# Joints of the last stages of a two-layer transformer kernel: who waits for scatters, which queues write the zero rows, when table words are loaded, and the first gathers of the second attention

## The chip, the cores and the metric

The kernel runs on one core of one Trainium2 chip. The core's engines are TensorE (PE in the profile, with PEld for its weight loads), VectorE (DVE), ScalarE (ACT), GpSimd (POOL) and SyncE (SP). An engine name with a q (POOLq, SPq) means the engine's own queue of instructions: its waits, branches, register loads and DMA issues. The metric is the time of one execution on the device in microseconds (us); lower is better.

## The reference

The input x is 8 sequences of 512 tokens of 128 floats. Four stages are added to it, each on its layer norm:

```python
x = x + attn0(ln(x))   # 16 heads of 8; sum of a windowed (128), a strided (4) and a full softmax, times 1/3, @ w_out
x = x + ffn0(ln(x))    # 7 experts of 512, top 2 per token (SwiGLU), plus one shared expert for all tokens
x = x + attn1(ln(x))   # 16 heads of 8, rotary q and k, causal softmax, @ W_out
x = x + ffn1(ln(x))    # 8 experts of 256, top 2 per token, one after the other:
# gates = softmax(x @ gate_W + gate_b); e1, e2 = top-2 experts of a token, with weights w1, w2
# o1 = relu(x @ W1[e1] + b1[e1]) @ W2[e1] + b2[e1];  boost = x + 0.5 * o1
# o2 = the same of boost with expert e2;  result = layernorm(x + w1 * o1 + w2 * o2) * gamma + beta
```

## The kernel before

The program is a row of blocks. Each block has one instruction list for each engine; between blocks stands a joint: every engine runs to the end of its list and executes a DRAIN, all meet at a barrier, GpSimd clears the block's semaphores, and all meet again. These instructions carry the line of the block's `with nc.cleanup_on_exit()`: L60 for an attention, L1585 for the routing of the first mixture, L1974 for its expert pass, L2147 for each of the two expert passes of the second mixture.

The order of the blocks is: setup; attention 0; routing and shared expert of mixture 0 (`route_and_share`); its expert pass over 70 blocks of 128 token rows (`routed_pass`); attention 1, which also routes mixture 1 (`attention(..., causal=True, due, gate)`); expert pass 0 and expert pass 1 of mixture 1 (`expert_pass`, r = 0 and 1), 39 blocks of 128 rows each.

**Attention 1.** Events for all engines are written out in one list (`order`); `walk` gives each engine the events for which it has a handler, so each engine meets them in that order. It works on 8 sequences, b = 0 to 7, each as 4 tiles of 128 tokens and 4 groups of heads. Before sequence b is normed, the two expert results of each of its tokens are added to X: GpSimd issues one gather with add for each tile t and each of the two results j (`early` for b = 0, 1 and the first half of 2; `results` later). j = 1 of a tile may start only when j = 0 of that tile has landed. Before the change the wait stands ahead of the four gathers of j = 1 and asks for all four of j = 0:

```python
def early(b, turn, j):
    if j:
        pool.wait_ge(s_yg[b], 16 * NT)
    for t in range(NT):
        ...
```

The list begins with early(0,0), two memsets on VectorE (`ones`, L604 and L606), early(0,1), the norm of b = 0, early(1,0), early(1,1), the preparation of q, k and v for b = 0, the norm and the preparation of b = 1, and only then the first score maxima (`smax`, on TensorE and VectorE) and the slots of the pipeline.

**Routing of mixture 1.** For each sequence: `g_norm` (VectorE statistics, GpSimd's power, L1147 and L1149), `g_shift` (VectorE, L628), `g_rows` (ScalarE: one activation that writes token numbers, L993, and four that write the normed rows, L996), `g_beta` (GpSimd, L1157: X plus beta into the same row buffer), `g_turn`, `g_logits`, `g_soft`, `g_count`, `g_place`, `g_put`, and `scatter`, one indirect DMA for each tile from GpSimd into the DRAM tensor `rows_1` (L1175). For b = 0 to 6 these lie between the slots; for b = 7 they come one after the other at the end. `finish` then pads each expert's last block: SyncE loads eight addresses into registers and issues eight writes of 128 zero rows (L1240, L1241), waits for them and for the weights (L1242, L1243), VectorE makes the table of blocks, and GpSimd waits for its scatters (L1180).

**Expert passes.** SyncE reads the 128 rows of block i (L2203) and, in pass 0, now and then a block of zero rows for pass 1 (L2206). TensorE transposes them, ScalarE copies the expert's weights and the transposed rows (L2253, L2255), TensorE multiplies (L2229), ScalarE and VectorE apply the relu, TensorE multiplies again (L2237, L2240), VectorE combines (L2319, L2323, L2325; in pass 1 also the layer norm, of which the last step is L2311), and GpSimd scatters the rows to their places (L2333), in pass 0 into `rows_2` and in pass 1 into the output. Which expert a block has stands in a table in SBUF, four blocks to a word. `words` loads all ten words into registers ahead of the loop, on TensorE, ScalarE and, in pass 0, VectorE (`value_load`, L2180: a TENSOR_LOAD, register operations and an assertion each). In pass 0 VectorE also makes the table of pass 1, in parts, one in each of the first iterations (`next(later, None)`, all shown at L1411). At the end of a pass GpSimd waits for its scatters, one semaphore for each of the 16 row buffers (L2345).

**`routed_pass`** of mixture 0 loads its words inside the loop: one in every fourth iteration, on TensorE, ScalarE and VectorE, ahead of the weight copies (L2057, L2076).

## Time and profile before

| | |
|---|---|
| median of 3 runs | 1601.72 us (1600.91 to 1602.95) |
| profiled execution, its own time | 1599.95 us |
| its span, first to last instruction | 1598.2 us |
| attention 0 | about 15 to 626 us |
| mixture 0, routing and pass | 626 to 749 and 749 to 953 us |
| attention 1 with routing | 953 to 1452 us |
| expert pass 0, expert pass 1 | 1452 to 1524 and 1524 to 1598 us |
| busy share: PE, DVE, ACT, POOL | 86%, 67%, 56%, 41% |
| mean granted TensorE clock | 0.94 |

A row of the timeline gives the start in us, how long the instruction (or the run of xN instructions) took in us, the engine, the line, the operation with its output and inputs, and in brackets how long the engine sat idle before it and what released it. "issue" means that it waited for nothing that the profile shows. A row of the view of one line gives the shortest, median and longest duration in ns and the first and the last start in us. DRAIN, EVENT_SEMAPHORE and TENSOR_LOAD rows belong to an engine's queue and are not counted as busy.

### The profile page before, as it was taken

How to read it: one execution, taken by the hardware profiler on the slowest of the kernel's cores; microseconds unless marked ns; L12 is line 12 of the kernel's file. 1: busy time of each engine (PE TensorE's matmuls, PEld its weight loads, DVE VectorE, ACT ScalarE, POOL GpSimd, SP SyncE). 2: the span in 40 equal slices, each digit the busy share in tenths (PEclk: the TensorE clock that was granted, in tenths of full speed). 3: DMA queues.
4: the chain of work that ended last, by engine and by line, in shares of the span. 5: the costliest groups of instructions: out<-in, count | busy, mean ns of one | idle time of the engine just before them, and what ended most of it. 6: DMA issues, size and time to landing. Idle time of an engine off the chain costs nothing. (4 is left out here: it accounts for less than half of the span.)

```text
span 1598.2 us, 36810 instructions
## 1 busy us (share of the span) xinstructions
PE 1377.7 (86%) x12519; PEld 924.5 (58%) x12646; DVE 1068.3 (67%) x2710; ACT 894.7 (56%) x1594; POOL 654.2 (41%) x984
## 2 busy tenths in 40 slices
PE   2799999999999997998999972899999999944866
PEld 1255555555555554766999971355555555534866
DVE  4678778787877763674444444677787887844656
ACT  1567676767767665622444430366666666632666
POOL 2223332323333222055333326656667553342736
PEclk8699999999999998999999995799999999976978
DMA  4211212112121102350111113333433222205653
GB/s 128 66 42 38 59 41 63 53 37 63 35 59 43 62 6 92 90 85 14 49 50 48 49 33 55 84 82 70 113 79 102 71 89 72 68 35 157 213 144 106
DMA packets 91848, 113.65 MB, mean 71 GB/s; under 512 B 13075, under 2 KB 75570, under 8 KB 91538
## 3 DMA queue, kind: packets, MB, share of 16 engines
q1 hardware_dynamic: 74930, 89.74, 19.9%
q0 software_dynamic: 16736, 21.55, 5.7%
q8 instruction: 106, 1.74, 0.5%
q14 instruction: 76, 0.62, 0.1%
HBM read 71.78 MB, written 38.95 MB: 69 GB/s over the span
## 5 line engine op out<-in xcount | busy, mean ns | idle before, releaser
L522 DVE TENSOR_REDUCE wm<-wsm 128x16 f32<-128x512 f32 x512 | 330.1, 685 | 112.4 <-PE wsm L770 109.5
L956 ACT ACTIVATE we<-wst 128x1024 f32<-128x1024 f32 x320 | 325.1, 1023 | 119.9 <-PE wst L803 109.1
L518 DVE TENSOR_REDUCE cnm<-csm 128x1 f32<-128x512 f32 (+3 forms) x352 | 213.8, 637 | 49.4 <-PE csm L767 47.2
L956 ACT ACTIVATE ce<-cst 128x896 f32<-128x896 f32 (+1 forms) x256 | 173.7, 699 | 113.9 <-PE cst L798 75.5
L770 PE MATMUL wsm<-wks,wqs 96*128 96x512 bf16 x512 | 172.1, 391 | 9.8 <-DVE wm L522 6.2
L763 PE MATMUL csm<-cks,cqs 96*128 96x256 bf16 (+3 forms) x512 | 131.8, 309 | 13.8 <-DVE cnm L518 10.1
L803 PE MATMUL wst<-wqs,wks 128*128 128x512 bf16 x417 | 128.3, 383 | 13.3 <-issue 12.0
L2033 PE MATMUL abup<-abxt,abws 128*128 128x128 f32 x1120 | 138.5, 278 | 0.4 <-ACT abxt L2059 0.4
L2033 PEld LDWEIGHTS abup<-abxt,abws 128*128 128x128 f32 x1120 | 132.4, 194 | 0.7 <-ACT abxt L2059 0.7
L837 PE MATMUL woa<-we,wv 128*32 128x128 f32 (+2 forms) x2560 | 130.5, 340 | 0.0
L1058 POOL TENSOR_TENSOR wdif<-wglb,wloc 128x16 f32<-128x16 f32 x32 | 7.1, 221 | 289.7 <-DVE wloc L544 289.7
L2081 DVE TENSOR_TENSOR abht<-absg,abup 128x512 f32<-128x512 f32 x70 | 48.1, 688 | 101.6 <-ACT absg L2064 101.6
L795 PE MATMUL cst<-cqs,cks 128*128 128x384 bf16 (+3 forms) x480 | 112.4, 296 | 2.7 <-ACT ce L956 0.7
L2097 POOL DMA_INDIRECT axb<-rows,asource x67 | 66.1, 986 | 117.2 <-DVE abys L2088 112.7
L1131 POOL TENSOR_SCALAR_AFFINE_SELECT ce<-ce 128x256 f32<-128x256 f32 x128 | 65.3, 539 | 92.8 <-ACT ce L956 92.5
L770 PEld LDWEIGHTS wsm<-wks,wqs 96*128 96x128 bf16 x512 | 49.7, 98 | 88.0 <-DVE wm L522 51.7
L2064 ACT ACTIVATE absg<-abup 128x512 f32<-128x512 f32 x70 | 41.8, 597 | 102.5 <-PE abup L2033 102.5
L837 PEld LDWEIGHTS woa<-we,wv 128*32 128x32 f32 x2560 | 66.8, 109 | 52.7 <-issue 36.4
L763 PEld LDWEIGHTS csm<-cks,cqs 96*128 96x128 bf16 x512 | 45.8, 101 | 76.3 <-DVE cnm L518 43.2
L767 PE MATMUL csm<-const_b 128*128 128x128 bf16 (+2 forms) x352 | 88.0, 250 | 0.0
L829 PE MATMUL coa<-ce,cv 128*32 128x512 f32 (+3 forms) x1024 | 82.7, 441 | 0.7 <-ACT ce L956 0.6
L803 PEld LDWEIGHTS wst<-wqs,wks 128*128 128x128 bf16 x512 | 39.7, 101 | 63.1 <-ACT we L956 25.4
(330 smaller groups left out, 3012.3 us busy)
## 6 DMA issues: line engine op xcount, KB each, us to landing
wqs<-qk_parts SPq DMA_DIRECT2D x96, 96.0 KB
wks<-qk_parts SPq DMA_DIRECT2D x96, 96.0 KB
cqs<-qk_parts SPq DMA_DIRECT2D x96, 96.0 KB
cks<-qk_parts SPq DMA_DIRECT2D x96, 96.0 KB
b1r<-rows SPq DMA_DIRECT2D x39, 194.0 KB, 2.7
qk_parts<-wpt SPq DMA_DIRECT2D x48, 128.0 KB
qk_parts<-cpt SPq DMA_DIRECT2D x48, 128.0 KB
b0r<-rows SPq DMA_DIRECT2D x39, 130.0 KB, 2.5
```

Source lines behind the costliest of these rows:

```text
L518: dve.tensor_reduce(NM[:, n % 2, first:first + heads, t], got, AX.X, ALU.max).then_inc(s_mx, 1)
L522: dve.tensor_reduce(M[:, n % 2, hs, t, :].rearrange("p (w f) -> p w f", f=DIL), SM[:, j % 2, :].rearrange("p (w i f) -> p w f i", w=NT, f= ...
L763: pe.matmul(sm[:, i * keys:(i + 1) * keys], QS[0:MR0, h, t * P:(t + 1) * P], KS[0:MR0, h, 0:keys], start=(i == 0), stop=False, skip_group_ ...
L767: pe.matmul(own, const["later_b"], ident, start=False, stop=True, skip_group_check=True).then_inc(s_sm, 1)
L770: pe.matmul(sm, QS[0:MR0, h, t * P:(t + 1) * P], KS[0:MR0, h, :], start=True, stop=True, skip_group_check=True).then_inc(s_sm, 1)
L795: m = pe.matmul(st[:, at:at + width], KS[:, h, kb * P:(kb + 1) * P], QS[:, h, kb * P:S], start=True, stop=not masked, skip_group_check=True)
L803: m = pe.matmul(st[:, c * S:(c + 1) * S], KS[:, h, kb * P:(kb + 1) * P], QS[:, h, :], start=True, stop=True)
L829: m = pe.matmul(OA[VW * hs:VW * (hs + 1), S - width:S], V[:, kb, g * HG + hs, 0:VW], E[:, e_slot(g, HG * r + hs), at:at + width], start=(k ...
L837: m = pe.matmul(span(OA[VW * hs:VW * (hs + 1), :], a, z), V[:, r, g * HG + hs, col:col + VW], span(e, a, z), start=(r == 0 and a == 0), st ...
L956: act.activation(E[:, e_slot(g, i), 0:width], ST[:, (U * g + i) % 2, 0:width], ACT.Exp, scale=SCALE).then_inc(s_ex, 1)
L2033: m = pe.matmul(UP[:, i % 2, w, c * P:(c + 1) * P], WS[:, i % 2, w, c * P:(c + 1) * P], XT[:, i % 2, :], start=True, stop=True)
L2097: pool.indirect_dma_start(XB[:, q, :], None, rows, bass.IndirectOffsetOnAxis(ap=source[:, i:i + 1], axis=0)).then_inc(s_in[q], 16)
```

## The change

Five edits are made.

1. Scatters: the waits for GpSimd's scatters at the end of attention 1, of pass 0 and of pass 1 move from GpSimd's list to SyncE's.
2. Zero rows: of the eight writes of `finish`, SyncE loads and issues the even four and ScalarE the odd four, on ScalarE's own DMA queue.
3. Words: four words (`SOON1`) are loaded ahead of the loop of an expert pass, the other six inside it, one at the head of each iteration until all ten are known, on TensorE, ScalarE and (pass 0) VectorE.
4. First gathers: for b = 0 and 1 a new semaphore for each tile, `s_y0[t]`, lets the j = 1 gather of tile t wait for the j = 0 gather of that tile alone. The counts that `norm_stats` and `results` wait for on `s_yg[0]` and `s_yg[1]` are lowered to match.
5. Routing rows: ScalarE writes the token numbers after the four row activations instead of before them, and `g_beta` on GpSimd waits for `g_shift` on VectorE as well.

```diff
@@ -151,6 +151,7 @@
             s_yg = [sem(f"yg{i}") for i in range(4)]
+            s_y0 = [sem(f"y0{t}") for t in range(NT)]
         if gate:
@@ -450,7 +451,7 @@
                 if due:
-                    dve.wait_ge(s_yg[b % 4], 16 * 2 * NT * (b // 4 + 1))
+                    dve.wait_ge(s_yg[b % 4], 16 * 2 * NT * (b // 4 + 1) - (16 * NT if b % 4 < 2 else 0))
                 if causal and b > 2:
@@ -990,12 +991,12 @@
                 room(act, b)
-                act.activation(ROWS[:, rows_of(b), IN_TOKEN].bitcast(U32), const["steps"][:, b * NT:(b + 1) * NT], ACT.Identity,
-                               bias=const["row"]).then_inc(s_gtok, 1)
                 for t in range(NT):
...
                 m.then_inc(s_grow, 1)
+                act.activation(ROWS[:, rows_of(b), IN_TOKEN].bitcast(U32), const["steps"][:, b * NT:(b + 1) * NT], ACT.Identity,
+                               bias=const["row"]).then_inc(s_gtok, 1)
 
@@ -1006,6 +1007,12 @@
                     act.activation(route.V[:, 0:T, :], route.V[:, 0:T, :], ACT.Exp).then_inc(s_gex, 1)
+
+            def finish(b, turn):
+                act.wait_ge(s_r, marks["padded"])
+                for e in range(1, NE1, 2):
+                    at = act.value_load(route.PAD[0:1, 0, e:e + 1], min_val=0, max_val=TOP * CAP - P)
+                    act.dma_start(gate.rounds[0][bass.ds(at, P)], gate.ZE[:, 0:IN_ROW]).then_inc(s_pad, 16)
 
@@ -1016,24 +1023,26 @@
                            rows=rows, scores=scores, evac=evac, heads_T=heads_T, g_rows=g_rows, g_turn=g_turn, g_soft=g_soft,
-                           g_put=g_put))
+                           g_put=g_put, finish=finish))
 
...
                 if j and t == 0:
-                    pool.wait_ge(s_yg[b % 4], 16 * 2 * NT * (b // 4) + 16 * NT)
+                    pool.wait_ge(s_yg[b % 4], 16 * 2 * NT * (b // 4) + (0 if b % 4 < 2 else 16 * NT))
                 at = bass.IndirectOffsetOnAxis(ap=due[0][:, j, b * NT + t:b * NT + t + 1], axis=0)
...
             def early(b, turn, j):
-                if j:
+                if j and b > 1:
                     pool.wait_ge(s_yg[b], 16 * NT)
                 for t in range(NT):
+                    if j and b < 2:
+                        pool.wait_ge(s_y0[t], 16 * (b + 1))
                     at = bass.IndirectOffsetOnAxis(ap=due[0][:, j, b * NT + t:b * NT + t + 1], axis=0)
                     pool.indirect_dma_start(X[:, b * NT + t, :], None, due[1], at, compute_op=ALU.add
-                                            ).then_inc(s_yg[b], 16)
+                                            ).then_inc(s_yg[b] if j or b > 1 else s_y0[t], 16)
 
@@ -1153,6 +1162,7 @@
                 pool.wait_ge(s_res, b + 1)
+                pool.wait_ge(s_gsh, b + 1)
                 room(pool, b)
@@ -1175,12 +1185,8 @@
 
-            def finish(b, turn):
-                for i in range(RING1):
-                    pool.wait_ge(s_sc[i], 16 * NT * len(range(i, B, RING1)))
-
             walk(pool, dict(results=results, early=early, fill=fill, norm_rows=norm_rows, join=join, left1=left1, left2=left2, vcopy=vcopy, sel=sel, maxima=maxima, scores=scores,
-                            loads=loads, g_norm=g_norm, g_beta=g_beta, g_put=g_put, scatter=scatter, finish=finish))
+                            loads=loads, g_norm=g_norm, g_beta=g_beta, g_put=g_put, scatter=scatter))
 
@@ -1236,10 +1242,12 @@
                 sp.wait_ge(s_r, marks["padded"])
-                for e in range(NE1):
+                for e in range(0, NE1, 2):
                     at = sp.value_load(route.PAD[0:1, 0, e:e + 1], min_val=0, max_val=TOP * CAP - P)
...
                 sp.wait_ge(s_gw, 16 * 7)
+                for i in range(RING1):
+                    sp.wait_ge(s_sc[i], 16 * NT * len(range(i, B, RING1)))
                 sp.wait_ge(s_pad, 16 * NE1)
@@ -1370,6 +1378,7 @@
 USED1 = 39
+SOON1 = 4
 RING1 = 3
@@ -2180,7 +2189,11 @@
         def words(eng):
-            return [word(eng, at) for at in range(-(-N // UN))]
+            return [word(eng, at) for at in range(SOON1)]
+
+        def more(eng, known):
+            if len(known) * UN < N:
+                known.append(word(eng, len(known)))
 
@@ -2206,6 +2219,8 @@
                 sp.wait_ge(s_pad, 16 * NE1)
+            for q in range(Q):
+                sp.wait_ge(s_out[q], 16 * len(range(q, N, Q)))
 
@@ -2218,6 +2233,7 @@
             for i in range(N + 1):
+                more(pe, known)
                 if i + 1 < N:
@@ -2245,6 +2261,7 @@
             for i in range(-1, N + 3):
+                more(act, known)
                 if i + 1 < N:
@@ -2279,6 +2296,7 @@
                 if not final:
+                    more(dve, known)
                     next(later, None)
@@ -2341,8 +2359,6 @@
                 scatter(i)
-            for q in range(Q):
-                pool.wait_ge(s_out[q], 16 * len(range(q, N, Q)))
 
```

## Rows read from the trace of the kernel before

**Rows 1.** Busy time by engine, of 100 us in the middle of attention 1.
```profile
1100.00:1200.00 100.00, 93.14 (x840) 54.71 (x845) 82.50 (x203) 63.15 (x113) 65.10 (x82) 1.00 0.36 90
```

**Rows 2.** Timeline of GpSimd, first gathers of attention 1.
```profile
963.09 1.53 POOL L1035 DMA_INDIRECT X<-results,slots  x1 [1.98 <-DMA X<-results,slots]
...
984.23 1.55 POOL L1035 DMA_INDIRECT X<-results,slots  x1 [2.09 <-DMA X<-results,slots]
...
990.54 1.55 POOL L1035 DMA_INDIRECT X<-results,slots  x1 [0.30 <-issue]
```

**Rows 3.** Timeline of VectorE in the same stretch.
```profile
959.37 6.88 DVE L606 MEMSET cks<- 64x8192 bf16 x1 [1.66 <-issue]
...
994.52 0.87 DVE L457 BATCH_NORM_STATS2 cstats<-X 128x6 f32<-128x128 f32 x4 [5.71 <-DMA X<-results,slots]
```

**Rows 4.** Line L628 over the whole run: count, durations in ns.
```profile
L628 DVE SCALAR_TENSOR_TENSOR cgsh<-cgmv,cgrs x8: 295/328/1158, 1091.3 to 1422.9; 128x4 f32<-128x4 f32 x8
```

**Rows 5.** Timeline, routing of the last sequence.
```profile
1422.80 1.25 POOL L1157 TENSOR_TENSOR brows<-X,bbe 128x512 f32<-128x512 f32 x1
1422.92 1.16 DVE L628 SCALAR_TENSOR_TENSOR cgsh<-cgmv,cgrs 128x4 f32<-128x4 f32 x1 [1.53 <-POOL cgrs L1149]
1424.11 0.30 ACT L993 ACTIVATE brows<-const 128x4 uint32<-128x4 f32 x1 [6.90 <-DVE cgsh L628]
```

**Rows 6.** Timeline, end of attention 1 and start of pass 0.
```profile
1436.94 8.98 SPq L1241 DMA_DIRECT2D rows<-bze  x8
...
1441.05 0.96 POOL L1175 DMA_INDIRECT rows<-brows,bIDX  x1 [0.31 <-issue]
...
1452.73 2.95 SPq L2203 DMA_DIRECT2D b0r<-rows  x4
```

**Rows 7.** Queue instructions of four joints, DRAIN on GpSimd, durations in ns.
```profile
L60 POOLq DRAIN  x1: 6591/6591/6591, 1444.1 to 1444.1; - x1
...
L2147 POOLq DRAIN  x3: 46/133/3244, 1519.4 to 1523.4; - x3
...
L1585 POOLq DRAIN  x3: 40/106/4800, 743.8 to 749.1; - x3
...
L1974 POOLq DRAIN  x3: 40/97/6711, 928.9 to 952.6; - x3
```

**Rows 8.** Timeline of GpSimd, the last indirect DMA ahead of three joints.
```profile
745.89 0.94 POOL L1962 DMA_INDIRECT axb<-rows,asource  x1 [0.30 <-issue]
...
929.10 0.94 POOL L2097 DMA_INDIRECT axb<-rows,asource  x1 [1.85 <-DVE abys L2088]
...
1516.69 0.98 POOL L2333 DMA_INDIRECT rows<-b0r  x1 [0.30 <-issue]
```

**Rows 9.** Line L2180 over the run: word loads of two engines, ns.
```profile
L2180 PEldq TENSOR_LOAD <-bTAB x20: 295/300/557, 1451.9 to 1529.6; - x20
...
L2180 DVEq TENSOR_LOAD <-bTAB x10: 297/304/450, 1451.9 to 1457.4; - x10
```

**Rows 10.** Timeline of TensorE, first transposes of the two passes.
```profile
1458.75 0.69 PE L2216 MATMUL b0tx<-const,b0r 128*128 128x128 f32 x2 [24.22 <-issue]
...
1530.20 0.68 PE L2216 MATMUL b1tx<-const,b1r 128*128 128x128 f32 x2 [17.86 <-issue]
```

**Rows 11.** Page, DMA issues: KB each, median us from issue to landing.
```profile
b1r<-rows SPq DMA_DIRECT2D x39, 194.0 KB, 2.7
...
b0r<-rows SPq DMA_DIRECT2D x39, 130.0 KB, 2.5
```

**Rows 12.** Timeline of VectorE in the pass of mixture 0, with and without a word.
```profile
806.52 0.43 DVE L2076 COPY abws<-awu 128x512 f32 x1 [0.42 <-issue]
...
808.81 0.42 DVE L2076 COPY abws<-awu 128x512 f32 x1
```

**Rows 13.** Timeline of GpSimd, where the unbroken run of scatters begins in each pass.
```profile
1472.83 0.99 POOL L2333 DMA_INDIRECT rows<-b0r  x1 [0.81 <-DVE b0r L2323]
...
1541.71 0.98 POOL L2333 DMA_INDIRECT out<-b1r  x1 [24.04 <-DVE b1r L2311]
```

## The prediction

> **What bounds the kernel now.** I read the busy time by stage first. In the middle of attention 1 TensorE is busy 93% of the time and VectorE 82% [rows 1]; the change removes nothing there. It touches the places where these engines stand still: the start of attention 1, the routing of the last sequence, the three joints and the first iterations of the passes. So I went through those with the timeline of all engines, asking which instruction ends last, and took the queue instructions of the joints line by line.
>
> At the start of attention 1 VectorE waits for the gathers: its statistics for b = 1 begin when the last gather has landed, after 5.71 us of idle time [rows 3]. At the end of attention 1 the zero-row writes are issued by 1436.94 + 8.98 = 1445.9, and the last scatter by 1442.0 [rows 6], but GpSimd's DRAIN runs from 1444.1 for 6.59 us, to 1450.7 [rows 7]. That DRAIN is what the joint waits for. The joint after pass 0 is alike: last scatter issued by 1517.7 [rows 8], DRAIN 1519.4 to 1522.6 [rows 7]. In the passes GpSimd sets the pace once it has caught up: from 1472.83 in pass 0 and from 1541.71 in pass 1 [rows 13] the scatters follow one another every 0.98 + 0.30 us or so without a break (34 and 38 intervals). Whatever comes earlier ahead of these two points comes earlier at the end of the pass.
>
> **Part 1, first gathers.** The fifth gather waited 1.98 us instead of the 0.30 of its neighbours, and in b = 1 2.09 us [rows 2]: 1.68 + 1.79 = 3.47 us of waiting on GpSimd. With a semaphore for each tile nothing of it should be left: a gather lands at most 4.0 us after it starts (990.54 to 994.52 [rows 2, 3]), and the gather that needs it comes four gathers later, at least 4 x (1.53 + 0.30) = 7.3 us. Queued behind the waits are the other gathers, the norm's power and the memset of v; all move up. VectorE's statistics for b = 1 wait for nothing but the last gather, so its norm, its projections and then the first maxima come 3.5 us earlier; b = 0 needs only 1.7 us of that, and its copies out and back lie ahead of the first maxima. I take 3.5; the bounds are 3.5 and 0, if the pipeline of attention 1 is paced by something that did not move. The new semaphores cost one wait each of a value already reached.
>
> The fifth gather now falls at 961.4, inside VectorE's memset (959.37 to 966.25 [rows 3]). The old one, at 963.09, did too, and took the same 1.53 us as those outside it [rows 2]. The Trainium skill (SBUF — State Buffer, "SBUF: two separate sides") says that GpSimd cannot write its DMA descriptors while VectorE holds the shared port pair in a 2-port mode. By that rule the fifth gather would stand until 966.25; the row of 963.09 does not show it for this memset. It is a rival below.
>
> **Part 2, routing rows.** `g_shift` takes 328 ns as a median of eight and 1158 ns once [rows 4]: the last time, when it runs beside GpSimd's L1157 (1422.80, 1.25 us) and ends with it [rows 5]. The added wait puts L1157 behind it: 1.16 - 0.33 = 0.83 us, on the path, since ScalarE's rows, the logits, the choice and the scatters of b = 7 all follow. The token numbers (0.30 us [rows 5]) go behind the rows: I take 0.2, as neighbouring ScalarE rows overlap; bounds 0 and 0.3. L1157's 1.25 us are hidden: the first use is the scatter at 1436.8, and GpSimd idles until then. For b = 0 to 6 `g_shift` stands seven events ahead of `g_beta`, so its wait is free. Sum 1.0 (0 to 1.1).
>
> **Part 3, zero rows on two queues.** Four writes instead of eight end SyncE's issuing near 1441 instead of 1445.9. GpSimd's DRAIN hides both; I count 0, for both bounds. Without that cover the edit would be worth up to 4.9 us. ScalarE has nothing else to do there.
>
> **Part 4, who waits for the scatters.** GpSimd reaches its DRAIN without waiting for landing. What does such a DRAIN take? Two joints show it [rows 7, 8]: the last gather ends at 746.83 and the DRAIN at 743.8 + 4.80 = 748.6, 1.8 us later, with 3 indirect DMAs in the block; and 930.04 to 928.9 + 6.71 = 935.6, 5.6 us later, with 67 in the block. Slope (5.6 - 1.8) / 64 = 0.059 us for each. The DRAINs behind a wait have the same slope: 6.59 us with 96 (64 gathers, 32 scatters), 3.24 with 39, 3.35 / 57 = 0.059. So I estimate 1.8 + 36 x 0.059 = 3.9 us after the last scatter's issue in a pass and 1.8 + 93 x 0.059 = 7.3 us in attention 1:
> - attention 1: 1442.0 + 7.3 = 1449.3 instead of 1450.7, 1.4 us;
> - pass 0: 1517.7 + 3.9 = 1521.6 instead of 1522.6, 1.0 us;
> - pass 1, which ends in the same way: 1.0 us.
>
> Sum 3.4. Lower bound 0, if the DRAIN's end hangs on the landing; upper bound, the old DRAIN directly behind the issue: 1448.6 and twice 1520.9, 2.1 + 1.7 + 1.7 = 5.5. SyncE's waits end where GpSimd's did, by 1444.1 and 1519.4, and lie under the DRAIN.
>
> **Part 5, words.** In pass 0 the first load starts at 1451.9 and VectorE's tenth at 1457.4, 0.61 us each [rows 9]; TensorE's ten end by 1458.75, 0.68 each [rows 9, 10]. With four words TensorE is ready at 1454.6; block 0's rows land at 1452.73 + 2.5 = 1455.2 [rows 6, 11]. Lead: 1458.75 - 1455.2 = 3.5 us. In pass 1 TensorE's last load starts at 1529.6 [rows 9], so the first at about 1523.7; the read comes 0.83 later as in pass 0 and lands after 2.7 [rows 11], at 1527.3: lead 1530.20 - 1527.3 = 2.9.
>
> Against it stand six loads in the loop. A word in a loop costs VectorE 0.42 us of idle time where it has none without [rows 12]. In pass 0 five of them (with `later`'s table work between) lie ahead of the fifth scatter, where the unbroken run begins: 5 x 0.42 = 2.1 if nothing absorbs them. VectorE still has small gaps there, so 1.7 are lost, and 1.8 are left (bounds 3.5, all hidden, and 3.5 - 5 x 0.61 = 0.4). In pass 1 VectorE has no words; on TensorE and ScalarE the loads lie behind multiplications and activations already issued. I take 0.1 us for each of five, 2.4 left (bounds 2.9 and 2.9 - 5 x 0.68 = -0.5).
>
> **Sum.** 3.5 + 1.0 + 0 + 3.4 + 1.8 + 2.4 = 12.1 us. The profiled execution's span becomes 1586.1 and its own time 1599.95 - 12.1 = 1587.8; the median of the runs is 1.8 above it, so 1589.6.
>
> **Rivals.**
> - *Loads in the loop cost in full (slower).* TensorE, ScalarE and VectorE hand each block on in a ring. If each load (0.68, about 0.6, 0.61) lies on that ring, five iterations cost 5 x 1.9 = 9.5 in pass 0 and 5 x 1.3 = 6.5 in pass 1, 16.0 against a lead of 6.4; with the other parts' 7.9 the sum is +1.7: 1603.4. It turns slower from about 1.4 us an iteration. Rows 12 speak against it. 4%.
> - *The start of attention 1 is absorbed*, by copies of q and k or by gathers of later sequences that pace it: 1593.1. TensorE's 93% speak against it. 15%.
> - *The words bring nothing*, because VectorE's table work in pass 0 and a later rise of TensorE's clock eat the lead: 1593.8. 12%.
> - *The moved wait does not do what it says*: DRAIN still ends a fixed time after landing: 1593.0. 8%.
> - *VectorE's memset holds back the early gather*: it starts at 966.25 instead of 963.09, 3.2 lost instead of 1.7 won: 1594.5. 2%.
> - Two of the middle three together: near 1597, 6%; all three: 1601, 4%.
>
> The forecast itself has 49%. A difference of 0.2% (3.2 us) is about what a measurement of this kernel can tell from no change. The cases above that bound are the first (4%, slower) and those within it the last one and part of the pairs (6%): faster 90%, same 6%, slower 4%. All bounds taken for the good give 3.5 + 1.1 + 5.5 + 3.5 + 2.9 = 16.5: 1585. The range reaches up to the pairs: 1585 to 1597.
>
> **What would show it.** The fifth gather near 961.4 with 0.30 idle, and statistics of b = 1 near 991. `g_shift` at 0.33 in all eight. GpSimd's DRAIN beginning before its last scatter has landed, ending 3.9 and 7.3 us after the issue. First transposes 3.5 us after the first word load instead of 6.9, and scatter five of pass 0 only 1.8 us closer to the barrier. The prediction is wrong if the slots of attention 1 do not keep the 3.5 us, if the DRAINs end as late as before, or if the first iterations of the passes stretch.

## The result and the profile after

| | before | after |
|---|---|---|
| median of the runs, us | 1601.72 | 1585.18 (5 runs, 1582.70 to 1587.47) |
| ratio, 95% interval | | 0.9895 [0.9881, 0.9909] |
| profiled execution, its own time, us | 1599.95 | 1585.6 |
| its span, us | 1598.2 | 1583.9 |

The change makes the kernel 16.8 us faster (1601.72 x 0.0105; 14.6 to 19.1 by the interval). The forecast was 12.1 us, and the 16.5 us of "all bounds for the good" come nearest. A second series of the changed kernel in another group of runs (e9 below) gave 1583.24 and 0.9887 [0.9872, 0.9901]. Two of the ten runs of e7 below had a mean granted clock of 0.901 instead of 0.944 and took 1593.9 and 1599.8 us, which widens its interval.

Start of attention 1: the timeline of GpSimd after the change, then that of VectorE, to be laid beside [rows 2, 3].

```profile
962.69 1.53 POOL L1044 DMA_INDIRECT X<-results,slots  x1 [0.30 <-issue]
...
982.14 1.82 POOL L1044 DMA_INDIRECT X<-results,slots  x1 [0.30 <-issue]
```
```profile
960.64 6.88 DVE L607 MEMSET cks<- 64x8192 bf16 x1 [1.66 <-issue]
...
992.39 0.87 DVE L458 BATCH_NORM_STATS2 cstats<-X 128x6 f32<-128x128 f32 x4 [4.95 <-DMA X<-results,slots]
```

Both waits of 1.98 and 2.09 us have become 0.30. The blocks ahead, which the change does not touch, end 1.27 us later in this execution, so 962.69 stands for the 961.4 of the prediction. The fifth gather lies wholly inside the memset and takes the same 1.53 us as its neighbours: the rival in which the memset holds it back is refuted here. The rule of the Trainium skill that the prediction named (SBUF — State Buffer, "SBUF: two separate sides") is for VectorE operations in a 2-port mode, and no row says that this memset is one. Had it held the port pair, the gather would have stood until 967.5.

Routing of the last sequence: the timeline of all engines after, beside [rows 5, 6].

```profile
1422.91 0.16 DVE L629 SCALAR_TENSOR_TENSOR cgsh<-cgmv,cgrs 128x4 f32<-128x4 f32 x1 [1.53 <-POOL cgrs L1158]
1423.11 1.65 ACT L995 ACTIVATE brows<-X,cgsh,cgrs 128x128 f32<-128x128 f32 x4 [5.72 <-DVE cgsh L629]
1423.21 1.27 POOL L1167 TENSOR_TENSOR brows<-X,bbe 128x512 f32<-128x512 f32 x1 [0.40 <-issue]
...
1434.51 0.25 POOL L1173 TENSOR_SCALAR brows<-bDEST 128x4 uint32<-128x4 f32 x1 [10.03 <-DVE bIDX L1420]
1435.89 1.08 POOL L1185 DMA_INDIRECT rows<-brows,bIDX  x1 [1.13 <-issue]
1437.27 1.26 POOL L1185 DMA_INDIRECT rows<-brows,bIDX  x1 [0.30 <-issue]
...
1440.40 0.96 POOL L1185 DMA_INDIRECT rows<-brows,bIDX  x1 [0.30 <-issue]
```

`g_shift` takes 0.16 us instead of 1.16, and GpSimd's addition starts behind it. From `g_shift` to the destinations the chain takes 11.60 us (1434.51 - 1422.91) instead of 12.76. The scatters then give part of it back: from the destinations to the start of the last one it takes 5.89 us instead of 5.37 (the first starts 0.3 us later behind the destinations, the second takes 1.26 us instead of 0.98).

The joints: queue instructions of their lines after, DRAIN on GpSimd, durations in ns, beside [rows 7].

```profile
L60 POOLq DRAIN  x3: 46/171/10547, 1437.1 to 1448.5; - x3
L60 SPq COMPARE_BRANCH  x1: 41/41/41, 1443.4 to 1443.4; - x1
...
L2156 POOLq DRAIN  x6: 46/136/9166, 1508.8 to 1583.6; - x6
```

The DRAIN of attention 1 now begins at 1437.1, before the last scatters are issued, and ends at 1437.1 + 10.55 = 1447.66: 6.3 us behind the end of the last scatter's issue (1441.36), where it ended 8.7 behind it before. SyncE, which holds the waits now, is through at 1443.4, under the DRAIN. In pass 1 the last scatter's issue ends at 1579.65 and the DRAIN, 1573.7 + 9.17, at 1582.9: 3.2 us instead of 5.04.

The passes: TensorE's first transposes, then the fifth and the last scatter of each pass on GpSimd, beside [rows 8, 10, 13].

```profile
1451.85 0.48 PE L2231 MATMUL b0tx<-const,b0r 128*128 128x128 f32 x1 [18.50 <-DMA b0r<-rows]
...
1517.90 0.48 PE L2231 MATMUL b1tx<-const,b1r 128*128 128x128 f32 x1 [10.61 <-DMA b1r<-rows]
```
```profile
1465.58 0.99 POOL L2351 DMA_INDIRECT rows<-b0r  x1 [0.82 <-DVE b0r L2341]
...
1509.47 0.98 POOL L2351 DMA_INDIRECT rows<-b0r  x1 [0.30 <-issue]
...
1534.30 0.98 POOL L2351 DMA_INDIRECT out<-b1r  x1 [0.30 <-DVE b1r L2329]
...
1578.67 0.98 POOL L2351 DMA_INDIRECT out<-b1r  x1 [0.30 <-issue]
```

What released the first transposes has changed from "issue" to the landing of block 0's rows: TensorE waits for data now, where its own word loads had kept it. The rows of before for pass 1 are these: the fifth and the last scatter, and the DRAINs of both passes. Behind pass 1 the DRAIN ran from 1594.0 to 1597.2.

```profile
1546.98 0.98 POOL L2333 DMA_INDIRECT out<-b1r  x1 [0.30 <-DVE b1r L2311]
...
1591.17 0.98 POOL L2333 DMA_INDIRECT out<-b1r  x1 [0.30 <-issue]
```
```profile
L2147 POOLq DRAIN  x6: 46/130/3244, 1519.4 to 1597.9; - x6
```

The fifth scatter of pass 0 comes 7.25 us earlier, that of pass 1 12.7 us. The unbroken runs behind them keep their length: 43.89 us (43.86 before) and 44.37 (44.19).

### The profile page after: what moved, and what is told of

It is laid out like the page before. It is cut to its first block and busy times, and to the rows that moved or that the text cites. A ratio compares the mean times of both kernels' runs of the same rounds, so it can differ in the third digit from the quotient of the medians.

```text
span 1583.9 us, 36812 instructions
## 1 busy us (share of the span) xinstructions
PE 1378.5 (87%) x12519; PEld 922.1 (58%) x12646; DVE 1066.5 (67%) x2710; ACT 895.2 (57%) x1594; POOL 654.2 (41%) x984
```

## How the stages were compared

A single pair of profiles is a poor ruler here. Attention 1 from its first to its last eviction of the output weights (ScalarE's rows that write `cos`, 32 in each profile) takes 376.05 us in the profile of before and 378.63 in that of after. Read alone, this pair says that 2.6 of the 3.7 us won at the start are given back, and that was my first reading. In this stretch the kernels differ by edit 5 at most (e4, with edit 5 alone, took 377.2 us). It took 376.0 to 379.8 us in the six profiles with the old first gathers (mean 377.7) and 374.4 to 379.7 in fourteen with the new ones (mean 377.2). So nothing is given back on average, as far as means that move by about a microsecond can tell, and what one profile says of this stretch is uncertain by some 2.5 us. The stages below are measured from one event to the next, which takes the drift of the stages ahead out.

The first blocks of a pass drift too, for a reason that the profile shows. TensorE's granted clock stands at the lower level (PEclk 0.50, 1.2 GHz) when the first transposes run. It rises to the upper one (1.00, 2.4 GHz) 3.5 to 7.3 us behind them in pass 0 (e12, an experiment on it, apart), and the place changes from profile to profile. In pass 1 of the ten profiles at 1.29 us a block the fifth scatter comes 16.1 to 16.3 us behind the first transposes where the clock rises 4.4 to 5.0 us behind them, and 16.8 to 17.0 where it rises 6.3 to 6.7 us behind them, whichever kernel it is. In the profile of before the rise is late in both passes (6.5 and 6.7 us).

In the groups of e1 to e4, e13 to e16 and e17 to e18 the kernel before itself took 1638, 1642 and 1640 us. In all profiles of these groups 34 blocks of a pass took 58.1 to 63.1 us, 1.71 to 1.85 us a block instead of 1.29: most scatters still follow one another at 1.29 us, but about every third interval takes 2.4 to 3.6 us, with idle time that the profile puts to nothing. It is not the clock, since e18 ran its 34 blocks of pass 0 at a granted clock of 1.00. Times are compared only within a group, and beyond the fifth scatter of pass 0 the stages of these groups are uncertain by 2 us or more, as such pauses fall into them.

## Experiments

**One part alone, in the kernel before (e1 to e4; before in this group 1638.16 us).** The edits are the hunks of the diff: e1 the first gathers, e2 the waits for the scatters, e3 the words, e4 the routing rows. Only the telling lines of each are shown, cuts marked by "...".

```
 def early(b, turn, j):                      # e1
-    if j:
+    if j and b > 1:
         pool.wait_ge(s_yg[b], 16 * NT)
     for t in range(NT):
+        if j and b < 2:
+            pool.wait_ge(s_y0[t], 16 * (b + 1))
...
```
```
...
-            for q in range(Q):              # e2, GpSimd
-                pool.wait_ge(s_out[q], 16 * len(range(q, N, Q)))
+            for q in range(Q):              # e2, SyncE
+                sp.wait_ge(s_out[q], 16 * len(range(q, N, Q)))
...
```
```
-            return [word(eng, at) for at in range(-(-N // UN))]     # e3
+            return [word(eng, at) for at in range(SOON1)]
...
+                more(pe, known)
...
```
```
...
                 pool.wait_ge(s_res, b + 1)   # e4
+                pool.wait_ge(s_gsh, b + 1)
```

> The kernel before with edit 4 alone (a semaphore for each tile for the first gathers of attention 1). By the prediction's term: 3.5 us faster, kept to the end of attention 1. By the other theory, that attention 1 gives most of it back in stalls of its own: first score maxima 3.5 us or more nearer to the first gather, but the last sequence's normalisation only about 1.3 us nearer, and a time 1 to 2 us below before.

e1: 1634.45 us, ratio 0.9970 [0.9956, 0.9985], 4.9 us (2.5 to 7.2). From the first gather to the first eviction the stretch takes 79.72 us; it took 82.7 to 84.0 in the six profiles with the old gathers and 79.3 to 79.9 in the fourteen with the new. Means 83.3 and 79.6: 3.7 us. The gain by time is the prediction's 3.5 kept, not the 1 to 2 us of the other theory.

> The kernel before with edit 1 alone (SyncE waits for the scatters at the ends of attention 1 and of both passes). By the prediction's term: GpSimd's DRAINs end 7.3 us after the last scatter's issue in attention 1 and 3.9 us in each pass, 3.4 us faster. By the other theory, that a DRAIN takes the same time whether or not the scatters have landed, so that the landing is hidden whole: 6.3 us and 3.2 us after the issue, about 5.9 us faster.

e2: 1633.85 us, 0.9970 [0.9958, 0.9983], 4.9 us (2.8 to 6.9). From the last scatter of attention 1 to the fifth of pass 0 it takes 28.98 us, where e1 and e4 of this group take 30.58 and 31.31 and the profile of before 31.78: 1.6 to 2.8 us, in one joint. The time lies between the forecast's 3.4 and the other theory's 5.9 and excludes neither. The DRAIN's row decides:

```profile
L60 POOLq DRAIN  x3: 46/165/10341, 1443.5 to 1454.6; - x3
```

It ends at 1453.8, 6.6 us behind the end of the last scatter's issue (1447.21) and not 7.3; in the passes it ends 3.25 us behind it and not 3.9.

> The kernel before with edit 3 alone (four words ahead of the loop, six inside). By the prediction's term: pass 0 gains 1.8 us and pass 1 2.4 us, 4.2 us in all, since loads in the loop cost 0.42 us each on VectorE. By the other theory, that the loads in the loop cost nothing and the full clock of TensorE comes earlier with the earlier first matmul: fifth scatter of pass 0 about 4 us and first scatter of pass 1 about 3.8 us nearer to the block's first word load, 7.9 us in all.

e3: 1632.66 us, 0.9959 [0.9947, 0.9971], 6.7 us (4.8 to 8.7). The same stretch takes 28.72 us, and from the last scatter of pass 0 to the fifth of pass 1 it takes 28.75, where e1 and e4 take 31.5 and 32.0. The interval excludes the forecast's 4.2; e10 below, where passes run at 1.29 us a block, does not.

> The kernel before with edit 5 alone (token numbers after the rows, g_beta behind g_shift). Both theories: 1.0 to 1.2 us faster, with g_shift of the last sequence at 0.3 us or less instead of 1.16 us. If the time does not move, the chain of the last sequence is not what ends attention 1.

e4: 1638.51 us, 0.9998 [0.9986, 1.0011]: the 1.0 to 1.2 us that were expected are not seen, and the runs could hardly resolve them. Its profile shows the same 11.59 us from `g_shift` to the destinations as the changed kernel, and the same 5.90 us from there to the last scatter. So it is this edit that makes the scatters slower, and its own balance is 1.17 - 0.53 = 0.6 us.

**Zero rows (e5: alone in before; e6: the changed kernel with all eight on SyncE again; before in this group 1601.36 us).**

```
-                for e in range(NE1):         # e5; e6 puts this back
+                for e in range(0, NE1, 2):
                     at = sp.value_load(route.PAD[0:1, 0, e:e + 1], min_val=0, max_val=TOP * CAP - P)
```

> The kernel before with edit 2 alone (ScalarE issues four of the eight zero-row writes). Prediction and rival alike say 0, because GpSimd's DRAIN ends last at that joint. A theory that the second queue disturbs the scatters gives 0.5 us slower: the four scatters then stand 1.5 us apart instead of 1.29 us.

e5: 1601.83 us, 1.0001 [0.9991, 1.0010].

> The changed kernel with all eight zero-row writes on SyncE again. If GpSimd's DRAIN, at 6.3 us after the last scatter, still covers SyncE's eight writes, the time is that of the changed kernel within 0.5 us. If the two queues matter now, the joint ends about 1 us or more later.

e6: 1586.47 us, 0.9909 [0.9892, 0.9925], beside 0.9895 and 0.9887 with four on each queue. SyncE's branch comes at 1445.6, GpSimd's DRAIN ends at 1447.05: still covered, and the first transposes come 11.3 us behind the last scatter, as in the changed kernel (11.4). The edit is worth nothing with either form of the joint.

**An early DRAIN (e7: in the changed kernel; e8: the same with eight zero rows on SyncE).**

```
 def g_beta(b, turn):
     ...
                                    across(gate.BE[:, :], [P, NT, D]), ALU.add).then_inc(s_gxb, 1)
+                if b == B - 1:
+                    pool.drain()
```

> The changed kernel with one more DRAIN on GpSimd in attention 1, right after g_beta of the last sequence, where GpSimd then idles about 10 us. Theory that a DRAIN's time goes by the number of indirect DMAs since the last DRAIN (about 0.055 us each): the extra one takes about 6 us, hidden, and the final one only about 2 us after the last issue instead of 6.3; then the landing of scatters and zero rows ends the joint, near 3 us after the last issue, and the time is 3 us below the changed kernel. Theory that it takes a fixed time in this block or goes by the traffic around it: the final DRAIN stays near 6.3 us and the time stays.

> The same extra DRAIN with all eight zero-row writes on SyncE. If the final DRAIN is short, SyncE's eighth write (issued near 5 us after the last scatter's issue starts, landing 2 us later) ends the joint and the run is 2 to 3 us slower than with two queues: the price of edit 2 once its cover is gone. If the DRAIN stays long, no difference.

The queue instructions of the joint, e7 and then e8:

```profile
L60 POOLq DRAIN  x3: 46/171/6666, 1432.9 to 1440.5; - x3
L60 SPq COMPARE_BRANCH  x1: 41/41/41, 1439.5 to 1439.5; - x1
```
```profile
L60 POOLq DRAIN  x3: 46/171/5877, 1433.8 to 1444.2; - x3
L60 SPq COMPARE_BRANCH  x1: 41/41/41, 1443.2 to 1443.2; - x1
```

e7: 1578.38 us, 0.9882 [0.9849, 0.9915]. The last DRAIN ends 2.7 us behind the last scatter's issue (1436.88 to 1439.57) instead of 6.3, a gain of 3.6. e8: 1583.26 us, 0.9889 [0.9873, 0.9906]: the DRAIN is over at 1439.7 there, and the joint waits for SyncE until 1443.2. The cover of edit 2 is gone, and its price appears: by the profiles 2.8 us from the last scatter to the first transposes (7.87 and 10.69) and 3.2 us to the fifth scatter of pass 0 (22.24 and 25.43). Between the medians it is 4.9. The prediction had "up to 4.9 us" for this case; that the medians differ by just this is chance, since the stage shows about 3.

**The changed kernel again, the words alone again, and the clock (e9 to e12; before in this group 1601.08 us).** e11 and e12 add matmuls at the start of each pass's list for TensorE, e12 has the early DRAIN too:

```
...
+            for _ in range(6):
+                pe.matmul(UP[:, 1, 1, :], const["ident_b"], const["wide_b"], start=True, stop=True)
             known = words(pe)
```

> The changed kernel once more, beside the three that follow, so that they are compared on one chip. Both theories expect the time it had: 1585 us where the kernel before takes 1601, a ratio of 0.988 to 0.991. It also shows how far the attention's length (first to last row of ScalarE's eviction of the output weights) moves between executions of the same code: so far 360.5 to 363.2 us.

e9: 1583.24 us, 0.9887 [0.9872, 0.9901].

> Edit 3 alone (four words ahead, the rest in the loop), on a chip whose expert passes run at the pitch that the prediction was made from, 1.29 us a block; where it was run first they took 1.78 us a block. Theory A (what the profiles show from the joint to the fifth scatter: 4.2 us in pass 0 and 3.8 us in pass 1): about 8 us below the kernel before. Theory B (the prediction's term): 4.2 us below. The passes' pitch in the loop should stay at 1.29 us a block by both; if the loads in the loop cost something it shows there.

e10: 1595.60 us, 0.9965 [0.9953, 0.9977], 5.6 us (3.7 to 7.5), which contains the forecast's 4.2 and leaves "about 8" just outside. First transposes, then fifth scatters of e10:

```profile
1457.35 0.48 PE L2221 MATMUL b0tx<-const,b0r 128*128 128x128 f32 x1 [20.11 <-DMA b0r<-rows]
...
1525.78 0.47 PE L2221 MATMUL b1tx<-const,b1r 128*128 128x128 f32 x1 [12.41 <-DMA b1r<-rows]
```
```profile
1471.73 0.99 POOL L2341 DMA_INDIRECT rows<-b0r  x1 [0.83 <-DVE b0r L2331]
...
1542.05 0.98 POOL L2341 DMA_INDIRECT out<-b1r  x1 [0.31 <-DVE b1r L2319]
```

In pass 0 the first transposes come 13.59 us behind the last scatter of attention 1 (1443.76) instead of 17.70, the fifth scatter 14.38 behind them instead of 14.08: 4.1 won, 0.3 lost. In pass 1 it is 10.21 behind 1515.57 instead of 13.51, then 16.27 instead of 16.78. So this pair shows 3.8 us in each pass, 7.6 in all. Part of it is not the edit: the DRAIN of e10's first joint ends 0.3 us sooner behind the last scatter, and the clock rises 1.7 and 2.1 us sooner behind the first transposes than in the profile of before. Measured from the end of the DRAIN, the first transposes come at 4.2 us instead of 8.0 in pass 0 and at 4.2 instead of 7.5 in pass 1, and all profiles agree within 0.4 us (but for the first joint of e8, which SyncE ends): a lead of 3.8 and 3.4, 7.2 us in all. What the reads in the loop take back is measured below.

> The changed kernel, with six matmuls of 128x512 (bf16) that write a bank of PSUM which the pass overwrites later, ahead of TensorE's first word in each pass: they run while its sequencer reads the words and waits for the rows. Theory A (part of the larger gain of edit 3 is that TensorE's granted clock rises earlier, because it works earlier, and that the first blocks run on it): the clock's rise moves up by 1 to 3 us against the first transposes, and the time falls by 1 to 3 us over both passes. Theory B (the start is bound by the rows' landing, the words and GpSimd, not by TensorE's rate): within 0.5 us of the changed kernel, or 1 us slower where the matmuls stand in the way of the first transposes.

> The same with GpSimd's early drain of the fourth experiment of the second group. Against the kernel with the six matmuls alone: theory A (the drain that the joint waits for costs by the scatters and gathers issued since the one before) 3.6 us less; theory B (the 6.8 us between the two medians came with the drain itself, by something that the profile does not show yet) 6 to 7 us less.

e11: 1584.00 us, 0.9891 [0.9878, 0.9905], no different from e9. e12: 1581.05 us, 0.9869 [0.9852, 0.9885]. TensorE's first rows, e11 and then e12:

```profile
1447.67 0.47 PE L2232 MATMUL b0tx<-const,b0r 128*128 128x128 f32 x1 [0.20 <-DMA b0r<-rows]
...
1448.85 1.06 PE L2248 MATMUL b0up<-b0xt,b0ws 128*128 128x128 f32 x4
...
1454.11 0.61 PE L2248 MATMUL b0up<-b0xt,b0ws 128*128 128x128 f32 x4
```
```profile
1446.63 0.33 PE L2234 MATMUL b0tx<-const,b0r 128*128 128x128 f32 x1 [0.23 <-DMA b0r<-rows]
...
1447.68 0.62 PE L2250 MATMUL b0up<-b0xt,b0ws 128*128 128x128 f32 x4
```

In e11 the clock of pass 0 still rises only 5.9 us behind the first transposes: four multiplications take 1.06 us until then, 0.61 afterwards. In e12 it has risen by the first transposes, and the first blocks run at the upper level from the start. From the first transposes to the fifth scatter that gives 12.99 us, where e7 and e15, with the early DRAIN and without the matmuls, took 14.37 and 14.19. So the clock in the first blocks is worth 1.2 to 1.4 us there. Whether it is kept that profile does not show: pass 0 behind its fifth scatter took 45.13 us instead of 43.9, by two single intervals of 1.66 and 2.20 us. It is too little to make 4.2 us into 7.6, but between two profiles whose clocks rise 2 us apart it moves the fifth scatter by up to 0.7 us. Against e11, the early DRAIN of e12 gives 2.95 us between the medians, in the size of theory A.

**Reads in the loop, words ahead, and the waits undone (e13 to e16; before in this group 1642.20 us).**

```
             if len(known) * UN < N:         # e13; e18 adds one read
+                for _ in range(2):
+                    word(eng, len(known))
                 known.append(word(eng, len(known)))
```
```
-SOON1 = 4                                   # e14
+SOON1 = 2
```

e15 is e7 once more; e16 is the changed kernel with e2's hunks taken out.

> The changed kernel, with each word that is read in the loop read three times, on TensorE, ScalarE and (in pass 0) VectorE: twelve reads more for each engine and pass, ten of them ahead of the fifth scatter. Theory A (the reads in the loop are nearly hidden): the fifth scatter of pass 0 comes at most 1.5 us later against the first transposes (13.7 to 14.4 us so far), pass 1 at most 1 us, the time 0 to 2.5 us more. Theory B (a read on VectorE costs 0.42 us and little of it is absorbed, as the prediction had it, and the larger gain comes from elsewhere): 10 x 0.42 = 4.2 us more in pass 0 and about 1 us in pass 1, so 5 us more. Theory C (each read lies on the ring of the three engines in full): 10 x 1.9 + 10 x 1.3 = 32 us more.

> The changed kernel with two words ahead of the loop instead of four. Theory A (the first transposes now wait for block 0's rows, whose read SyncE issues after its own word, so that fewer words ahead free nothing): first transposes at the same distance from the joint's end (4.2 us), time within 1 us of the changed kernel. Theory B (the words ahead still set the start): 2 x 0.65 = 1.3 us less in each pass, 2.6 us in all.

> The kernel with GpSimd's early drain once more. Theory A (3.6 us by the drain's rows; the rest of the first comparison was the attention's length, which moves by 2 us between executions of the same code): 2.5 to 4.5 us below the changed kernel, ratio to before 0.986 to 0.988 beside 0.9887 to 0.9895. Theory B (the whole 6.8 us is its own): 0.985 or less.

> The changed kernel without edit 1: GpSimd waits for its scatters again ahead of its drain, in attention 1 and in both passes. Theory A (a drain that starts at once ends 2.4, 1.7 and 1.8 us earlier): 5.9 us more than the changed kernel. Theory B (the prediction's sizes, 1.4, 1.0 and 1.0): 3.4 us more. Theory C (the joint ends a fixed time after the landing): no difference.

| | median us | ratio to before | last scatter of attention 1 to fifth of pass 0 | last of pass 0 to fifth of pass 1 |
|---|---|---|---|---|
| e13 | 1635.94 | 0.9968 [0.9953, 0.9982] | 32.87 | 31.78 |
| e14 | 1624.72 | 0.9903 [0.9883, 0.9922] | 25.81 | 28.31 |
| e15 | 1620.57 | 0.9880 [0.9858, 0.9903] | 21.87 | 26.31 |
| e16 | 1630.76 | 0.9935 [0.9913, 0.9957] | 27.64 | 28.33 |

e14 is like the changed kernel (25.18 and 25.23 us in its two profiles), with the first transposes 4.2 us behind the DRAIN's end in both: two words fewer ahead free nothing, since the landing of the rows now ends the wait. The changed kernel itself did not run in this group, so e14 serves as its reference. e16 is 6.0 us slower than it, beside theory A's 5.9; with intervals of 3 us each that favours it and does not exclude 3.4. Its joints say it more closely: 1.7, 1.8 and 1.8 us longer than e14's (last scatter to the first transposes 13.16 and 11.44, then 10.08 and 8.31, last scatter to the end of the span 6.98 and 5.20), 5.3 in all, and theory C is refuted. e15 is 4.2 us faster, again theory A of the drain, not 6.8. e13 falsifies my "nearly hidden": 11.2 us more. The two reads more cost 7 us in pass 0 alone, more than theory B had.

**The price of one, two and three reads (e17, e18; before in this group 1640.37 us).** e17 takes the reads in the loop out; the word comes from the four read ahead, so other experts are used from the seventeenth block on.

```
-                known.append(word(eng, len(known)))
+                known.append(known[len(known) % SOON1])
```

> The changed kernel without the reads in the loop: blocks from the seventeenth on take their expert's number from one of the four words read ahead, so that the experts (and the output) are others there; the work is the same. Theory A (one read in an iteration fits into the slack of the first blocks): from the first transposes of pass 0 to its fifth scatter 13.4 to 14.1 us as in the changed kernel (13.7), pass 1 as there (16.4), time within 1 us. Theory B (the reads cost what the prediction took, 1.7 and 0.5 us, and edit 3's lead is larger instead): 12.0 and 15.9 us, time 2.2 us less.

> The changed kernel with each word of the loop read twice. If the price is linear (7.1 us for ten reads more, 0.7 each): the same stretch of pass 0 takes 17.3 us, 3.6 more. If the first reads hide and only what goes beyond the slack is paid (theory A of the run without reads, taken further): under 2.5 us more here, and most of the 7 us with the third.

TensorE's first transposes and GpSimd's fifth scatter in pass 0, of e17, e18 and e13:

```profile
1452.39 0.48 PE L2231 MATMUL b0tx<-const,b0r 128*128 128x128 f32 x1 [18.44 <-DMA b0r<-rows]
...
1466.15 0.99 POOL L2351 DMA_INDIRECT rows<-b0r  x1 [0.80 <-DVE b0r L2341]
```
```profile
1450.49 0.48 PE L2232 MATMUL b0tx<-const,b0r 128*128 128x128 f32 x1 [18.40 <-DMA b0r<-rows]
...
1467.87 0.99 POOL L2352 DMA_INDIRECT rows<-b0r  x1 [1.93 <-DVE b0r L2342]
```
```profile
1453.94 0.47 PE L2233 MATMUL b0tx<-const,b0r 128*128 128x128 f32 x1 [18.41 <-DMA b0r<-rows]
...
1475.44 0.99 POOL L2353 DMA_INDIRECT rows<-b0r  x1 [2.08 <-DVE b0r L2345]
```

No read 13.76 us, one read 13.73, two 17.38, three 21.50. But the changed kernel's profile is the one in which the clock rises first of all. TensorE's clock (the number behind the counts, 0.50 or 1.00 at either level) from 3.5 to 6.0 us behind the first transposes, after and then e17:

```profile
1455.35:1457.85 2.50, 2.47 (x21) 2.27 (x21) 2.30 (x7) 1.91 (x7) 0.13 (x1) 1.00 0.50 131
```
```profile
1455.89:1458.39 2.50, 2.50 (x16) 2.50 (x15) 1.71 (x6) 1.08 (x4) 0.00 (x0) 0.58 0.55 141
```

So every profile goes into one table; the first number of each pair is how many us behind the first transposes of pass 0 the clock rises, the second how many behind them the fifth scatter starts.

| reads in an iteration | clock rise and fifth scatter, us |
|---|---|
| none, all ten words ahead | 4.2, 13.41 (e2); 4.3, 13.44 (e1); 4.6, 13.48 (e4); 5.0, 13.48 (e5); 6.5, 14.08 (before) |
| none, words reused | 5.6, 13.76 (e17) |
| one | 3.5, 13.73 (after); 3.9, 13.81 (e9); 4.5, 14.29 (e6); 4.8, 14.38 (e10); 5.2, 14.74 (e8); 5.9, 14.20 (e11); 6.2, 14.19 (e15); 6.5, 14.37 (e7); 6.7, 14.37 (e14); 6.7, 14.47 (e16); 6.9, 15.02 (e3) |
| two | 5.0, 17.38 (e18) |
| three | 7.3, 21.50 (e13) |

Where the clock rises at about the same place, the five first reads cost 0.3 to 0.9 us together, at most 0.2 us each. The second five cost 2.6 to 3.0 us, the third five up to 4.1 (less what the late clock of e13 costs): 0.5 to 0.8 us each, about the 0.61 that one read takes on VectorE. In pass 1, where VectorE reads nothing, the first reads cost nothing that can be told: 16.3 us without (e5, clock rising at 5.7) and 16.4 with (after, 5.8). Theory A holds nearly for one read and not beyond; my guess that the second would still hide in part was wrong, and the linear price (17.3 us) was right for it. VectorE's timeline of e17, after and e13 shows where idle time came from, each at the same step of the table work (in brackets the idle time ahead of it):

```profile
1460.96 0.10 DVE L1420 MEMSET bEJ<- 128x48 f32 x1
```
```profile
1460.37 0.10 DVE L1420 MEMSET bEJ<- 128x48 f32 x1 [0.25 <-issue]
```
```profile
1468.97 0.10 DVE L1420 MEMSET bEJ<- 128x48 f32 x1 [1.41 <-issue]
```

One read leaves VectorE idle for 0.25 us here, three for 1.41. The pass without reads has a wait of its own in these iterations (once 0.65 us for TensorE's product, where the changed kernel has none). That fits a first read that mostly replaces idle time and further ones that are paid; which engine's read is the one that is paid was not tried.

The times of e17 and e18, 1618.08 us (0.9860 [0.9844, 0.9876]) and 1629.80 (0.9945 [0.9931, 0.9959]), are 11.7 us apart. Of that, 3.6 and 2.4 us lie in the two stretches up to the fifth scatters (28.74 - 25.17 and 28.57 - 26.22); another part lies in the passes behind them, 60.4 and 58.7 us in e17 and 61.7 and 60.4 in e18, where e17 uses other experts. By the ratios e17 is also some 5 us below the changed kernel (0.9860 beside 0.9891, the mean of its two), which neither theory had; the changed kernel did not run in this group, and the other experts and the pauses stand in the way. What reads cost in passes at 1.78 us a block is not settled by this.

## Why the prediction was right and wrong

Every mechanism of the forecast is there, none of the rivals is, and the sum was too small: 12.1 us predicted, 16.8 measured. Two terms were too small, the waits and the words. By stages, from event to event, in us:

| stage | before | changed kernel | gain | predicted |
|---|---|---|---|---|
| first gather to first eviction of attention 1 | 83.3 (mean of 6) | 79.6 (mean of 14) | 3.7 | 3.5 |
| first to last eviction | 377.7 (mean of 6) | 377.2 (mean of 14) | not told from 0 | 0 |
| `g_shift` to the last scatter of attention 1 | 18.13 | 17.49 | 0.6 | 1.0 |
| last scatter to the fifth of pass 0 | 31.78 | 25.18, 25.23 | 6.6 | 1.4 + 1.8 |
| pass 0 behind it | 43.86 | 43.89, 43.86 | 0 | 0 |
| last of pass 0 to the fifth of pass 1 | 30.29 | 24.83, 24.95 | 5.4 | 1.0 + 2.4 |
| pass 1 behind it | 44.19 | 44.37, 44.36 | -0.2 | 0 |
| last scatter to the end of the span | 7.03 | 5.23 | 1.8 | 1.0 |

The gains add up to 17.9, beside 16.8 timed. The two rows on the first blocks hold about a microsecond of luck, since the only profile of before has the clock rising late in both passes. Put together term by term from all profiles it is 3.7 for the gathers, 0.6 for the routing rows, 5.3 to 5.9 for the waits and 6.3 to 6.9 for the words: 15.9 to 17.1.

- **First gathers: right.** 3.5 forecast, 3.7 found, and as far as the means can tell it reaches the end of attention 1. "The start of attention 1 is absorbed" (15%) is not borne out, though the single pair of profiles seemed to.
- **Routing rows: mechanism right, one term missing.** The chain gained 1.16 where 1.0 was written. The sum did not have that the scatters behind it take 0.52 us longer, which e4 shows with this edit alone.
- **Zero rows: right.** Nothing while the DRAIN covers them (e5, e6); about 3 us by the stages once it does not (e7, e8).
- **Waits for the scatters: mechanism right, size off.** The step that failed is "I estimate 1.8 + 36 x 0.059 = 3.9 us after the last scatter's issue in a pass and 1.8 + 93 x 0.059 = 7.3 us in attention 1". It is 3.2 and 6.3. Between these two the slope is (6.3 - 3.2) / 57 = 0.054 us for each indirect DMA, near the 0.059; the start of the sum, 1.8 us with 3 indirect DMAs, was carried over from the joint behind the routing of the first mixture, another kind of block, and does not fit these. The line through 3.2 and 6.3 gives 1.3 us for 3 or 4 and 4.7 for 67, where that joint had 1.8, the one behind the pass of mixture 0 had 5.6, and the DRAIN behind four scatters in e7, e12 and e15 2.5 to 2.7. So the count is not all that sets it, and what else does is open. The joints gain 2.4 (8.7 - 6.3), 1.7 and 1.8 us in the first pair, 5.9 instead of 3.4, and 5.3 in e16 against e14. That is about the 5.5 of the upper bound.
- **Words: the other term that was too small.** 1.8 + 2.4 = 4.2 stood against 6.3 to 6.9. The leads were nearly right: 3.5 and 2.9 forecast, 3.8 and 3.4 found. The step that failed is "VectorE still has small gaps there, so 1.7 are lost", with its 0.1 for each read in pass 1: the five reads cost 0.3 to 0.9 us in pass 0 and nothing that can be told in pass 1. The 0.42 us of [rows 12] is idle time of VectorE in another pass; I charged it to the path as if the path ran through VectorE in each of these iterations. The rows beside it in the profile of before speak against that:

```profile
805.16 0.69 DVE L2081 TENSOR_TENSOR abht<-absg,abup 128x512 f32<-128x512 f32 x1 [1.51 <-ACT absg L2064]
...
807.95 0.69 DVE L2081 TENSOR_TENSOR abht<-absg,abup 128x512 f32<-128x512 f32 x1 [0.99 <-ACT absg L2064]
...
810.74 0.69 DVE L2081 TENSOR_TENSOR abht<-absg,abup 128x512 f32<-128x512 f32 x1 [1.51 <-ACT absg L2064]
```

  Between the first two lies the word's 0.42 us, between the last two none, and both stretches take 2.79 us: VectorE's next wait, for ScalarE, is 0.99 instead of 1.51 us. The read was hidden there already, and the words beside it (795.2, 817.5, 828.6 and 839.8 us) leave 0.21 to 0.23 us, not 0.42.
- **The range.** Its lower end was the sum of all bounds for the good, and the result lies at it: 1585.18 by the median, and 16.8 us by the ratio beside 16.5. Two of the five terms came out at about the upper bound that I had given them (waits 5.3 to 5.9 beside 5.5, words 6.3 to 6.9 beside 3.5 + 2.9 = 6.4). The sum of all bounds is no rare meeting, then: the two sizes that were wrong carried it there.

What stays open: what besides the count sets the DRAIN's length; why the scatters become slower with the routing rows' edit; why the passes of some groups run at 1.78 us a block; and why the clock of e12 had risen by the first transposes and that of e11 had not, with the same six matmuls ahead.

The kernel with the early DRAIN beats both: 0.9882 (e7), 0.9869 (e12) and 0.9880 (e15), beside 0.9895, 0.9887 and, for e14, 0.9903. The comparisons inside a group give 2.2 (e12 and e9), 3.0 (e12 and e11) and 4.2 us (e15 and e14), the rows of the DRAIN 3.6. The 6.8 us between e7 and the changed kernel, which ran in different groups, were not seen again. In its own group e7 is 8.1 us below e6; of this 4.0 us lie in the stretch of attention 1 that no edit explains (374.4 and 378.4 in the two profiles) and 3.4 us between the last scatter and the fifth of pass 0.

## What to carry to other kernels

A wait moved off the engine whose cleanup closes a joint is worth what that cleanup can then overlap; look for what an engine still has to do behind its last wait, and whether part of it fits into an idle stretch ahead (here a DRAIN in some 10 us of idle GpSimd shortened the last one by 3.6 us). To price a small instruction that is to stand in a loop, take it out and double it: the first may cost little and the second its full time, and an edit that is covered has no price until its cover goes. An idle gap beside an instruction is not its price; look whether the engine's next wait is shorter by as much. Before a gain is read as given back, or an instruction as free, from one pair of profiles, the same stretch belongs measured in every profile at hand, with the place where the clock rises beside it.

## What the runs showed of the hardware that I had not expected

- GpSimd's DRAIN at the end of a block takes longer with more indirect DMAs issued in it (3.2 us behind the last issue with 39, 6.3 with 96), and it does not need them to have landed when it starts. With a DRAIN ahead of the last four scatters of 96, 6.3 us behind the last issue become 2.7.
- The four scatters of the last sequence took 5.9 us from the destinations to the last start instead of 5.4 once GpSimd's addition stood behind `g_shift`, and 5.4 again with a DRAIN between that addition and the scatters (e7: 1430.55 to 1435.92).
- The granted clock of TensorE rises 3.5 to 7.3 us behind the first transposes of pass 0, at a place that changes from profile to profile. Six matmuls of 128x512 ahead of them left it at the lower level (1.2 GHz) for another 5.9 us in one kernel (e11), and in the other (e12) the first transposes already ran at the upper one (2.4 GHz).
- The same stretch of attention 1, 377 us long, varies by 5 us from one profiled execution to another (e7 and e15, the same kernel: 374.4 and 379.7).
